# Moving two per-token normalizations from VectorE to ScalarE and GpSimd in the second attention of a two-layer transformer kernel

## The reference

```
x = x + L1_attn(layernorm(x))   # 16 heads of 8, causal softmax over
                                # q.k/sqrt(8) + incidence(read_line_q, write_line_k)
                                #               * decay_h**(q-k) * bias_h
x = x + L1_ffn(layernorm(x))    # router: layernorm(x) @ router_w, 8 experts, the best 2,
                                # softmax over the two, gelu MLP 128-512-128 per expert
```

## Time and profile before

| what | value |
|---|---|
| runs | 1814.32 us median of 3 (1808.61 to 1819.41) |
| profiled execution, span from its first to its last instruction | 1776.1 us |
| its own time | not given apart from the span; median less span is 38.2 us |
| second attention, with its router | from about 840 to 1586 us of the span |
| a turn of it (2 to 5) | about 86 us |
| busy over the span: TensorE, VectorE, ScalarE, GpSimd | 82%, 72%, 53%, 39% |
| busy from 840 to 1586 us, in the same order | 588, 583, 344 and 293 of 746 us |

### The profile page before, as it was taken

How to read it: one execution, slowest core, us unless ns; L and a number is a source line. 1 busy time by engine, 2 the same in 40 slices (tenths; PEclk the granted TensorE clock), 3 DMA queues, 4 the chain that set the end, 5 groups by cost and what they waited for, 6 DMA issues and landing times. The chain is left out here.

```text
span 1776.1 us, 37567 instructions
## 1 busy us (share of the span) xinstructions
PE 1455.7 (82%) x11726; PEld 964.8 (54%) x11726; DVE 1274.7 (72%) x3482; ACT 935.2 (53%) x1914; POOL 694.1 (39%) x812
## 2 busy tenths in 40 slices
PE   3999999999999729995378887878888887837993
PEld 1224334333343319994256766666666665627993
DVE  6777888888787435555777879697978786834555
ACT  2577777777775505662435455454545453314561
POOL 3122342633520334554233344444444541233552
PEclk8699999999998969997689999898999998978997
DMA  6211111111110332222544443434344434132225
GB/s 158 66 42 59 47 52 53 61 53 49 49 62 15 128 123 67 73 72 82 164 150 126 126 128 106 131 109 129 112 125 122 130 111 138 38 130 56 71 72 162
DMA packets 122418, 166.37 MB, mean 94 GB/s; under 512 B 21490, under 2 KB 96018, under 8 KB 121586
## 3 DMA queue, kind: packets, MB, share of 16 engines
q1 hardware_dynamic: 113330, 145.69, 28.1%
q0 software_dynamic: 8896, 18.30, 3.0%
HBM read 116.04 MB, written 47.60 MB: 92 GB/s over the span
## 5 line engine op out<-in xcount | busy, mean ns | idle before, releaser
L1124 DVE TENSOR_REDUCE a_M<-a_F 128x1 f32<-128x512 f32 x512 | 325.8, 683 | 90.0 <-PE a_F L1318 88.1
L1025 ACT ACTIVATE L_W<-a_ST 128x512 f32<-128x512 f32 x512 | 276.8, 595 | 89.1 <-PE a_ST L1359 88.3
L2028 ACT ACTIVATE L_W<-c_ST 128x1024 f32<-128x1024 f32 x160 | 163.3, 1021 | 188.4 <-PE c_ST L2408 141.1
L2630 ACT ACTIVATE L_hT<-L_P,L_W1s 128x128 f32<-128x128 f32 x600 | 171.5, 368 | 142.9 <-PE L_P L2711 110.6
L2616 POOL DMA_INDIRECT L_yd<-L_ys,L_di x150 | 163.1, 1087 | 151.6 <-DVE L_ys L2662 147.2
L489 POOL DMA_INDIRECT L_xd<-L_XN,L_place_i x128 | 124.4, 972 | 146.5 <-issue 131.9
L1359 PE MATMUL a_ST<-L_W 74*128 74x512 bf16 x512 | 168.9, 395 | 11.1 <-ACT L_W L1025 6.3
L1318 PE MATMUL a_F<-L_W 72*128 72x512 bf16 x512 | 167.1, 403 | 7.7 <-DVE a_M L1124 6.9
L2702 PE MATMUL L_P<-L_xT,L_W1s 128*128 128x128 f32 x1200 | 161.0, 278 | 0.0
L2711 PE MATMUL L_P<-L_W,L_hT 128*128 x1200 | 159.1, 276 | 0.1
L2407 PE MATMUL c_ST<-ident,c_SD 128*128 128x128 f32 x512 | 149.7, 292 | 5.5 <-ACT L_W L2028 5.5
(11 more groups left out here) (430 smaller groups left out, 3164.9 us busy)
## 6 DMA issues: line engine op xcount, KB each, us to landing
c_QS<-c_q SPq DMA_DIRECT2D x32, 504.0 KB
c_QS<-c_rd SPq DMA_DIRECT2D x32, 378.0 KB
L_xg<-L_xd SPq DMA_DIRECT2D x150, 64.5 KB
L_W<-a_q SPq DMA_DIRECT2D x32, 288.0 KB
L_W<-a_k SPq DMA_DIRECT2D x96, 96.0 KB
L_W<-c_k SPq DMA_DIRECT2D x96, 96.0 KB
L_W<-in_L_w SPq DMA_DIRECT2D x8, 1024.0 KB
c_QI<-c_r SPq DMA_DIRECT2D x32, 216.0 KB
```

Source lines behind the costliest of these rows:

```text
L1025: act.activation(PT[:, j, kk, :], ST[:, kk, :], ACT.Exp).then_inc(sem(exped), 1)
L1124: dve.tensor_reduce(M[:, t, h:h + 1], FB[n % BANKS][:, :], AX_X, ALU.max).then_inc(sem(maxed), 1)
L2028: act.activation(PT[:, j, :, :], ST[:, :, :], ACT.Exp).then_inc(sem(exped), 1)
L2630: act.activation(hT[:, n % 2, f, :], PS[2 + 2 * (n % 2) + f // 2][:, (f % 2) * P:(f % 2 + 1) * P], func, bias=W1s[:, n % WB, F + f:F + f + ...
```

## The change

In the turns, ScalarE applies both norms as Identity(scale * x + bias), with scale = rstd and bias = -mean * rstd for each token. GpSimd makes the bias in two more instructions each time (`norm_shift`, `shifted`). VectorE keeps the token numbers (`label`) and the statistics. On ScalarE the router's four 128x256 tiles stand at p = 15, ahead of the `r_turned` copy; the layer norm's four 128x128 tiles stand at p = 20. VectorE's `scale` behind `maxima` of head 1 in quad 2 is taken out, and `measure` gets a wait for the batch before to be applied. The layer norms of batches 0 and 1, ahead of the turns, stay on VectorE. Behind the last turn the router's norm of batch 7 goes to ScalarE too.

```diff
@@ class Route
+    def shifted(self, pool, i):
+        pool.tensor_scalar(self.ns[:, :], self.mv[:, :, 0], -1.0, None, ALU.mult).then_inc(sem(self.negated), 1)
+        pool.wait_ge(*turn(self.negated, i, 1))
+        pool.wait_ge(*turn(self.rooted, i, 1))
+        pool.tensor_tensor(self.ns[:, :], self.ns[:, :], self.rstd[:, :], ALU.mult).then_inc(sem(self.shift), 1)
+
+    def label(self, dve, i, opening):
+        dve.wait_ge(*turn(self.turned, i, 0))
+        if not opening:
+            dve.wait_ge(self.put[i % self.NB], 16 * CH * T * (i // self.NB))
+        dve.tensor_copy(self.XN[:, i % self.NB, :, :, D:ROW].rearrange("p t k o -> p t (k o)").bitcast(I32),
+                        self.dest[:, bass.ds(i * T, T), :]).then_inc(sem(self.scaled), 1)
+
+    def apply(self, act, i, opening):
+        act.wait_ge(*turn(self.shift, i, 1))
+        act.wait_ge(*turn(self.turned, i, 0))
+        if not opening:
+            act.wait_ge(self.put[i % self.NB], 16 * CH * T * (i // self.NB))
+        for t in range(T):
+            act.activation(self.XN[:, i % self.NB, t, :, 0:D], over(self.tile_of(i, t), 1, CH), ACT.Identity,
+                           scale=self.rstd[:, t:t + 1], bias=self.ns[:, t:t + 1]).then_inc(sem(self.scaled), 1)
@@ gpsimd
                         norm_root(pool, c, norm, i, 0)
+                        norm_shift(pool, c, norm, i, 0)
                     put(i - 4, range(CH * T))
...
                     r.root(pool, i - 2)
+                    r.shifted(pool, i - 2)
...
             r.root(pool, B - 1)
+            r.shifted(pool, B - 1)
@@ scalar
+            def scale(i):
+                act.wait_ge(*turn(turned, i, 0))
+                norm_apply(act, c, norm, i, 0, lambda t: XN[:, t, :],
+                           lambda t: X[:, bass.ds(i * T + t, 1), :].rearrange("p a d -> p (a d)"))
...
                     p = SPOTS * g + s
+                    if tail and p == 15:
+                        r.apply(act, i - 1, opening=(i < 3))
+                    if n2 and p == 20:
+                        scale(i + 2)
                     for use in pieces(p, tail, n1, n2, routed):
...
             evacuate(("at", -1, 0), B)
+            r.apply(act, B - 1, opening=False)
             evacuate(("r_turned", -1, 0), B)
@@ vector
             def measure(i):
+                dve.wait_ge(*turn(norm["out"], i, 0))
                 norm_measure(dve, c, norm, i, 0, lambda t: x_tile(i, t))
...
                         if (g, j) == (1, 2) and tail:
-                            route_scale(i - 1)
+                            route_label(i - 1)
...
-                        if (g, j) == (2, 1) and n2:
-                            scale(i + 2)
...
-            route_scale(B - 1)
+            route_label(B - 1)
```

More of the change, by code:

```diff
@@ L260, in __init__ @@
         self.rstd = sb("rrstd", [P, T])
+        self.ns = sb("rns", [P, T])
         self.pad = sb("rpad", [P, 1])
@@ L314, in signals @@
         self.scaled = sig("r_scaled", T + 1)
+        self.negated, self.shift = sig("r_negated"), sig("r_shift")
         self.turned, self.copied, self.logits = sig("r_turned"), sig("r_copied"), sig("r_logits")
@@ L1526, in layer1_attention @@
         norm = norm_signals(sig, 1)
+        norm.update(negated=sig("norm_negated"), shift=sig("norm_shift"))
+        c = dict(c, ns=sb("ns", [P, T]))
         turned, xT = sig("turned"), sig("xT")
@@ L1797, in _ @@
             norm_root(pool, c, norm, 0, 0)
+            norm_shift(pool, c, norm, 0, 0)
             pool.memset(identb[:, :], 0.0).then_inc(made, 1)
@@ L1879, in _ @@
             norm_root(pool, c, norm, 1, 0)
+            norm_shift(pool, c, norm, 1, 0)
             pool.wait_ge(mixed2, T * 2)
@@ L1890, in _ @@
             r.root(pool, B - 2)
+            r.shifted(pool, B - 2)
             put(B - 3, range(CH * T))
@@ L2066, in route_measure, with route_label @@
                 r.take_stats(dve, i)
-            def route_scale(i):
-                r.scale(dve, i, range(T), opening=(i < 2))
+            def route_label(i):
+                r.label(dve, i, opening=(i < 2))
             def x_tile(i, t):
```

## The result

Before took 1811.5 us (median of 4 runs, 1808.6 to 1819.4), after 1844.2 (median of 4, 1827.6 to 1849.0), which is 10 us above the prediction's range (1808 to 1834). The ratio is 1.0126, with a 95% interval of 1.0078 to 1.0174; it isn't the quotient of the two medians, which is 1.018 (32.7 us) and lies above that interval. The same pair on two more chips, with 10 and 12 runs of the changed kernel, gave 1.0119 [1.0079, 1.0159] and 1.0099 [1.0066, 1.0133], and there the quotient of the medians is 1.010 both times. So I take the cost of the change as 18 to 23 us by the three ratios, where the prediction had +11.3 us: right in sign, a little over half the size. Counted on the 1811.5 us of before, that would end at 1829 to 1834 us, inside the range; the ratios don't bear out the 10 us above it.

The account below looks back on a forecast made before the run. TensorE was taken as busiest, held by VectorE in quads 0 and 1 and by a chain through the lines' DRAM round trip. 7.7 + 1.1 + 2.5 = +11.3 us took 1814.3 to about 1825.5, range 1808 to 1834.

Parts of the forecast that it names:

- VectorE gives time back, and TensorE is ready about 2 us earlier: Quad 1: VectorE loses four operations, 2.23 us in turn 3, so TensorE is ready for `r_turned` about 2.1 us earlier.
- 2.04 us for four, 0.06 us to TensorE: ScalarE's four router-norm operations ahead of `r_turned` take 2.04 us (bounds 1.64 and 2.8); TensorE starts 0.06 us later.
- The transposes start 7.7 us later in all: At `r_turned`, TensorE waits because ScalarE begins the router's norm too late: 7.7 us over turns 1 to 6.
- The layer norm counts for nothing: Quad 2: VectorE's freed 1.15 us (six turns) are lost again in the "issue" wait at the next logits; counted as 0.
- GpSimd's two operations: Two small added operations, about 0.5 us each time in quads 1 and 2, covered by GpSimd's idle time; counted as 0.
- +1.1 us behind the last turn: Nothing hides GpSimd's added 0.5 us there, and ScalarE's 2.04 us replace VectorE's 1.53: +1.1 us.
- TensorE's clock, 2.5 us with bounds of 0 and 5.1: New waits before `r_turned` lower the clock in turns 1, 4 and 5, up to 1.7 us each; 2.5 us taken.
- A (VectorE's time comes back): Rival: ScalarE's work is ready when TensorE is, so the turns gain 10.9 us; -9.8 net, 1804.5 us, chance 0.13.
- B: Rival: delay ahead of p = 16 is absorbed by the lines' DRAM round-trip wait; +3.3 us, 1817.6 us, chance 0.22.
- C (+18.5 us): Rival: the four operations take 2.8 us and the clock falls in all three turns; 1832.8 us, chance 0.15.
- D: Rival: ScalarE's work fits, VectorE's time is lost elsewhere, only the last 1.1 us show; 1815.4 us, chance 0.05.

Follow-up runs that it names:

- e1: The kernel of before, unchanged, run again for a second profile on chip A; ratio to before 0.999.
- e4: The changed kernel with the router's norm back on VectorE, so only the layer norm is on ScalarE; chip A, ratio to before 0.998.
- e2: The changed kernel, unchanged, run again for a second profile on chip A; ratio to before 1.0119.
- e3: The changed kernel with the layer norm back on VectorE, so only the router's norm is on ScalarE; chip A, ratio to before 1.0111.
- e15: The changed kernel with only the layer norm on ScalarE, the router's norm on VectorE, on chip D; ratio to before 0.9993.
- e13: The changed kernel, unchanged, run again on chip D; ratio to before 1.0099.
- e14: The changed kernel with only the router's norm on ScalarE, the layer norm on VectorE, on chip D; ratio to before 1.0097.
- e7: The changed kernel with 36 unneeded TensorE products in turns 1 to 6 during the wait for ScalarE's router norm; chip B, ratio to before 1.0036.
- e6: The changed kernel with ScalarE's router norm in two halves, at p = 11 and p = 13; chip B, ratio to before 0.9942.
- e9: The changed kernel with the router's norm split over p = 11 and 13, as in e6, again on chip C; ratio to before 0.9894.
- e8: The changed kernel with ScalarE's four router-norm operations of turns 1 to 7 done twice; chip B, ratio to before 1.0207.
- e5: The changed kernel with ScalarE's four router-norm operations at p = 13 instead of p = 15; chip B, ratio to before 0.9969.
- e10: The split version of e9 with the layer norm of quad 2 back on VectorE; chip C, ratio to before 0.9974.

## Why the prediction was wrong in size

By its own steps. Chip A compares e1 and e4 with e2 and e3 (means), chip D e15 with e13 and e14; in the stages named here the layer norm's move makes no difference beyond what executions differ by.

1. *VectorE gives time back, and TensorE is ready about 2 us earlier*: right. Its waits for VectorE fell by 13.2 us in five turns, and from its arrival on it only waited for ScalarE.
2. *2.04 us for four, 0.06 us to TensorE*: right (2.06; 1332.18 to 1332.23). The Trainium skill, ScalarE: Activation LUTs, section What ACT_TABLE_LOAD costs, gives 186 ns plus 0.833 ns an element plus about 93 ns for each per-token operand, an estimate of 585 ns for this shape; the trace's 587 agrees.
3. *The transposes start 7.7 us later in all*: right. Between the two first traces it is 29.7 - 21.7 = 8.0 us, turn by turn 3.8, 0.2, 0.2, 1.6, 1.8, 0.5 and -0.1, where 3.05, 0.28, 0.28, 1.70, 1.84, 0.60 and 0 were forecast. On chip A it is 6.5 us, on D 7.9.
4. *The layer norm counts for nothing*: nothing else was seen for this change (e4, e14, e15), within the intervals given above.
5. *GpSimd's two operations*: 0, with no wait of ScalarE for them in the turns.
6. *+1.1 us behind the last turn*: right, 1.0 on chip A and 1.1 on D.
7. ***TensorE's clock, 2.5 us with bounds of 0 and 5.1***: **this is the step that failed.** The stretch behind the transposes grew by 49.95 - 43.95 = 6.0 us on chip A and by 53.95 - 46.4 = 7.6 on D, beyond the upper bound. Two readings behind the term were wrong. *Which turns*: I let the clock fall in turns 1, 4 and 5, for an unbroken idle time of 2.7 us "as turn 3 has". Turn 3 has none: its waits of 1.53 and 1.12 us are parted by 0.38 us of work, and the clock fell all the same. With the router's norm at p = 15 (after, e2, e3, e13, e14) every turn from 2 to 6 had the same 4.26 to 4.30 us before the transposes, with TensorE busy for 1.0 to 2.1 of them, since ScalarE's schedule is the same in all of them. So turns 2, 3 and 6, which I took as unchanged, mostly pay more as well (8.1 and 8.3 us in turns 2 and 3 of e13 beside 6.4 and 6.3 in e15, 8.0 in turn 6 of e2 beside 5.5 in e1). *How long*: I priced a fall at the one stretch of 3.4 us that I had read it from the earlier trace rows, 1.7 us. It reaches from the transposes through the scores into the values and costs up to 2.5 us (7.98 us at a clock of 0.67 in turn 4 of e3, beside 5.5) or 2.9 (8.37 us at 0.64 in turn 5 of e13). e7 takes this term away by itself and saves at least as much.

With the measured terms the sum is 6.5 + 6.0 + 1.0 = 13.5 us on chip A. The traces there differ by 17.6 us, but 4.1 of it lie ahead of the second attention, so the other 13.5 are this sum. On D it is 7.9 + 7.6 + 1.1 = 16.6 us, to which the quad 2 of e13 and e14 adds 6.0, a stage that I had put at 0 and for which I have no cause; the traces there differ by 21.4 us. The ratios give 21 us on A (interval 14 to 28) and 18 us on D (12 to 24). Some 7 us on A stay without a place, and D has some 5 too many; two traces in which quad 1 does the same work differ by as much there (e4 has 5.6 us more than e1).

Of the rivals, A (VectorE's time comes back) was the right reading of VectorE and the wrong one of this schedule: its -9.8 us is about what the kernel gives once ScalarE's work is moved to where ScalarE idles (-10 us in e6 on chip B, but -19 in e9 on C). Its condition, ScalarE through 2.1 us before `r_turned`, was stated and read as not met, and that was so. B is refuted by e8. C (+18.5 us) named the right size with half the right reason: not slower operations (+4.6 us there, 0 measured), but the clock. D is out, since TensorE waits for the new ScalarE work in the turns.

The Trainium skill, Perfetto Trace Analysis, section Optimizing Scalar/DVE Operations, also says that breaking up instructions may let work be done sooner where ScalarE or VectorE aren't saturated but cause bubbles on another engine. The four operations were separate already; here it was parting them over two idle places. e6 (0.9942) stands against e5 (0.9969), but the intervals overlap; only the traces show it, with 0.5 us a turn at the exponential of head 3.

## What to carry to other kernels

Here work moved to a less busy engine gained only when it was put where that engine idles and ended before the consumer arrived. So compare the end of the moved group with the consumer's new, earlier arrival. Where a new wait appears on TensorE, price the whole stretch behind it at the lower clock, in every turn that has the wait, less what those turns already pay. Two cheap tests separate the rest: the same work some pieces earlier, and the wait filled with harmless products.

## What was not expected of the hardware

On chips C and D, and in the trace of after, some waits of ScalarE and VectorE go on when the matmul that they wait for has ended by the trace, whose ends of matmuls are modelled. They last up to 8.4 us in the turns, and the trace labels them "remote". ScalarE and VectorE in turn 3 of e10 and e9:

```profile
1247.23 0.56 DVE L2187 TENSOR_REDUCE c_M<-c_PAST 128x1 f32<-128x384 f32 x1 [5.34 <-remote]
1247.33 0.60 ACT L1956 ACTIVATE c_XT<-c_PV 128x512 f32<-128x512 f32 x1 [8.27 <-remote]
```

```profile
1241.04 1.02 ACT L2072 ACTIVATE L_W<-c_ST 128x1024 f32<-128x1024 f32 x1 [5.69 <-remote]
1241.14 0.69 DVE L2188 TENSOR_TENSOR c_inc<-c_INC,c_table 128x512 f32<-128x512 f32 x1 [4.88 <-remote]
```

There are 25 to 34 such waits, 96 to 135 us over the engines, in after and e9 to e15, and none in before and e1 to e8. They stand at the same places in each turn, in the first attention too, and quad 2 takes 26.7 to 29.2 us in turns 2 to 5 instead of 21.8 to 25.9. e2, the same kernel as after and e13, has none, and e15, with the router's norm on VectorE, has 34. So neither the change nor its router part decides it; they go with the chips on which before takes 1820 us instead of 1780, though no trace of the unchanged kernel was taken there. What holds those matmuls back I can't tell from the traces. The first two traces differ by 66 us where the kernels differ by some 20, and after is 40 us longer than e2, of the same kernel: only repeated pairs on one chip gave the size.
